# One PSUM operand in each pass of the norm chain, and new orders on all five engines

## The chip, the cores and the metric

The kernel runs on one core of a Trainium2 chip. The metric is the device time of one launch in microseconds; the time before is the median of three runs. All data is fp32 but for a few bf16 tables and parts.

## The reference, cut to what matters

The first part is a global attention over x of 8 sequences x 512 tokens x 128 channels, whose result is added at the end. The change leaves it alone but for one shared helper. The second part, called the layers here, takes most of the time. It applies the following to each of the 8 sequences, six times over with other weights:

```
# one layer, x: 512 tokens x 128 channels, 16 heads of 64
t    = shift_tokens(x)                 # the upper 64 channels come from the token before
q,k,v = split(t @ Wqkv)
q    = rotary(q / |q| * q_scale) ; k = rotary(k / |k| * k_scale)
sim  = 8 * q k^T                       # windows of 32 tokens look at themselves and the window before
attn = softmax(masked sim)
x    = x + (attn v) @ Wo
xn   = (x' - mean(x')) / sqrt(var(x') + 1e-5) * g + b       # x' = shift_tokens(x)
a, gate = split(xn @ W1 + b1)
x    = x + (a * gelu(gate)) @ W2 + b2
```

Each token needs 32 reciprocal norms (16 heads of q and 16 of k) and one reciprocal standard deviation: 512 tokens on 128 partitions make 4 x 32 + 4 = 132 numbers on a partition. They are computed in one go by a start value from integer arithmetic on the float's bits and three Newton steps. This is the norm chain.

## The kernel before, in words

The layers run on items: item n is sequence n mod 8 in layer n div 8, so there are 48. Every engine runs the same software pipeline. Its program is a `body` that is written out for i = -1 to 51 by `bodies`; x_0 is item i, x_1 item i - 1 and so on to x_4, and x_ahead is item i + 1. A stage of the work on an item is a small function, and a body is a list of such calls: this list, written out by hand for each engine, is the order in which the engine takes its work. An engine never takes work out of this order. All dependencies are semaphores.

An item passes these stages; the names are those of the functions, the letter is the engine (P TensorE, V VectorE, A ScalarE, G GpSimd, S SyncE).

- `tokens` (A) copies x and its shifted half to xs. `project` (P, L922) has 16 tiles of q and k, 4 for each of the 4 units (a unit is 4 heads), into the two buffers of pj_ps. Each tile is squared by `squares` (A, L1219), then multiplied by the gain and both rotary tables by `products` (V, L1092), which frees the buffer. `rotate` (G, L1317 and L1318) joins products to rotated queries or keys.
- `square_sums` (P, L932) adds up squares by head in the first 128 columns of nq_ps. `copy_sums` (A), `sums_by_token` (P, L940, a transpose), and `variance` of the item three before (P, L946) prepare the 132 numbers per partition in nq_ps. `norms` (V, L1105) adds eps and calls `rsqrt` (L58 to L65), eleven passes that each wait for the one before.
- `widen_norms` (A), `spread_norms` (P, L960) and `scale_keys` (V, L1118) multiply the keys by their reciprocal norms. `queries` and `keys` (S) rearrange both by DMA. `scores` (P, L971), `mask_scores` and `score_maxima` (V), `less_max` and `scale_scores` (G, L1322 and L1329), `exponentials` (A, L1236), `prob_sums` (V), `normal_probs` (G) and `prob_blocks` (V, a block transpose) make the probabilities of a unit.
- `token_transposes` (P) and `copy_tokens` (A) prepare x by token. `attend` (P, L991) runs on four groups of 128 tokens, `take_u` (A, L1250) copies the eight results, and `combine` (P, L1003) applies the product of value and output weights for 16 heads into to_ps. `attention_sum` (V, L1152) adds it to x.
- `ffn_tokens` (A), `centred` (P), `centred_squares` (A), `variance`, then a later run of the norm chain, `spread_rstd` (P, L953) and `normalise` (V, L1113). `up` (P, L1020), `gates` (A, L1270, Gelu), `gated` (V, L1158) for three chunks, `down` (P, L1027) and `ffn_sum` (V, L1165).

Everything that TensorE gives to others besides projections, sums and to_ps goes through the two slots of pair_ps, taken in turns in TensorE's order: `slot` waits until the reader of the work two before in this ring has freed it. attend takes both. to_ps is one buffer for combine and down. u is one buffer, so that take_u of an item waits for the last head of the item before. Exp and Gelu lie in different tables of ScalarE, and a load stands in the program wherever the one follows the other; squares and copies do with either.

In TensorE's order before, combine stands whole (heads 0 to 15 among projects) in one body, and after sums_by_token and variance comes attend 0 of the next item, so that two projects, attend 1 and project 2 are what it has while VectorE is in the norm chain.

## Time and profile before

| | |
|---|---|
| median of 3 runs | 3736.9 us (3736.53 to 3740.85) |
| profiled execution | 3733.54 us, span 3731.8 us |
| TensorE, VectorE, ScalarE, GpSimd busy | 92%, 80%, 49%, 58% of the span |
| mean granted TensorE clock | 0.980 |
| transposes of sums (L940), once an item | first at 561.0 us, last at 3574.8 us |

The span is from the first instruction to the last. Busy times are shares of it. In the timeline a row is one or several equal instructions in succession: the start, the length, the engine and line, output and input, their number, and in brackets how long the engine was idle before it and who released it. TensorE's matmuls overlap, so the distance between two starts is what counts there.

### The profile page before, as it was taken

How to read it: one execution, taken by the hardware profiler on the slowest of the kernel's cores; microseconds unless marked ns; L12 is line 12 of the kernel's file. 1: busy time of each engine (PE TensorE's matmuls, PEld its weight loads, DVE VectorE, ACT ScalarE, POOL GpSimd, SP SyncE). 2: the span in 40 equal slices, each digit the busy share in tenths (PEclk: the TensorE clock that was granted, in tenths of full speed). 3: DMA queues.
4: the chain of work that ended last, by engine and by line, in shares of the span. 5: the costliest groups of instructions: out<-in, count | busy, mean ns of one | idle time of the engine just before them, and what ended most of it. 6: DMA issues, size and time to landing. Idle time of an engine off the chain costs nothing. (4 is left out here: it accounts for less than half of the span.)

```text
span 3731.8 us, 75598 instructions
## 1 busy us (share of the span) xinstructions
PE 3415.4 (92%) x30012; PEld 1688.8 (45%) x30012; DVE 2966.9 (80%) x3289; ACT 1832.7 (49%) x2692; POOL 2171.0 (58%) x1534
## 2 busy tenths in 40 slices
PE   5888876999999999999999999999999999999986
PEld 3222223445454545545454545545454545445443
DVE  6788847888888888888888888888888888888862
ACT  2577753454545445454545454454545454454532
POOL 2322225757666675757576666757676666667550
PEclk7899998999999999999999999999999999999998
DMA  6222132323232323333232323233332323232221
GB/s 203 72 51 59 34 99 65 72 65 73 69 78 68 81 60 71 72 80 75 63 75 68 75 69 81 63 69 75 80 76 60 77 65 77 70 79 65 65 50 46
DMA packets 178253, 270.37 MB, mean 72 GB/s; under 512 B 42480, under 2 KB 67184, under 8 KB 176240
## 3 DMA queue, kind: packets, MB, share of 16 engines
q1 hardware_dynamic: 174160, 251.10, 29.0%
q10 hardware_dynamic: 3744, 14.43, 1.1%
q8 instruction: 242, 3.96, 0.5%
q14 instruction: 107, 0.88, 0.1%
HBM read 44.49 MB, written 19.55 MB: 17 GB/s over the span
## 5 line engine op out<-in xcount | busy, mean ns | idle before, releaser
L1092 DVE SCALAR_TENSOR_TENSOR ly_prod<-ly_pj_ps,ly_few,ly_tables 128x1024 f32<-128x1024 f32 x768 | 955.9, 1271 | 225.3 <-ACT ly_sq L1219 220.4
L922 PE MATMUL ly_pj_ps<-ly_xs,ly_wqk 128*128 128x512 f32 x1536 | 804.0, 621 | 103.8 <-DVE ly_prod L1092 91.4
L1219 ACT ACTIVATE ly_sq<-ly_pj_ps 128x512 f32<-128x512 f32 x768 | 454.7, 600 | 883.9 <-PE ly_pj_ps L922 591.2
L1003 PE MATMUL ly_to_ps<-ly_u,ly_mvo 128*128 128x512 f32 x1536 | 725.3, 596 | 0.9 <-DVE x_all L1165 0.9
L1250 ACT COPY ly_u<-ly_pair_ps 128x1024 f32<-128x1024 f32 x384 | 373.8, 1013 | 396.2 <-PE ly_pair_ps L991 396.2
L1322 POOL TENSOR_TENSOR ly_sx<-ly_sx,ly_smax 128x1024 f32<-128x1024 f32 x192 | 365.2, 1902 | 239.7 <-DVE ly_smax L1132 239.6
L1317 POOL TENSOR_TENSOR ly_qr<-ly_prod 128x512 f32<-128x512 f32 x192 | 244.2, 1272 | 425.5 <-DVE ly_prod L1092 420.5
L922 PEld LDWEIGHTS ly_pj_ps<-ly_xs,ly_wqk 128*128 128x128 f32 x1536 | 261.5, 191 | 499.3 <-issue 271.7
L1334 POOL TENSOR_TENSOR ly_sx<-ly_sx,ly_rsum 128x1024 f32<-128x1024 f32 x192 | 363.2, 1902 | 166.8 <-DVE ly_rsum L1140 166.8
L1003 PEld LDWEIGHTS ly_to_ps<-ly_u,ly_mvo 128*128 128x128 f32 x1536 | 280.5, 190 | 310.2 <-issue 310.2
L991 PE MATMUL ly_pair_ps<-ly_pt,ly_xt 32*128 32x512 f32 x3072 | 389.0, 620 | 25.7 <-ACT ly_u L1250 12.8
L971 PEld LDWEIGHTS ly_pair_ps<-ly_kbd,ly_qp 128*32 128x32 f32 x12288 | 325.6, 110 | 160.7 <-issue 157.9
L971 PE MATMUL ly_pair_ps<-ly_kbd,ly_qp 128*32 128x128 f32 x12288 | 376.7, 275 | 14.7 <-DMA ly_kbd<-ly_kr 14.6
L1329 POOL TENSOR_TENSOR ly_sx<-ly_sx,ly_rn 128x1024 f32<-128x1024 f32 x192 | 365.2, 1902 | 28.4 <-POOL ly_sx L1322 1.3
L1317 POOL TENSOR_TENSOR ly_kr<-ly_prod 128x512 f32<-128x512 f32 x192 | 247.3, 1288 | 209.1 <-DVE ly_prod L1092 206.2
L606 ACT ACTIVATE ga_pt<-ga_s_ps 128x512 f32<-128x512 f32 x512 | 276.9, 595 | 112.9 <-PE ga_s_ps L332 112.9
L466 DVE TENSOR_REDUCE ga_mx<-ga_f_ps 128x2 f32<-128x1024 f32 x256 | 302.5, 1220 | 35.9 <-PE ga_f_ps L312 34.8
L1020 PE MATMUL ly_pair_ps<-ly_xn,ly_w1c 128*128 128x512 f32 x576 | 288.8, 625 | 29.5 <-DVE ly_xn L1113 21.6
L1125 DVE TENSOR_TENSOR ly_sx<-ly_pair_ps,ly_mask 128x1024 f32<-128x1024 f32 x192 | 234.5, 1221 | 76.6 <-PE ly_pair_ps L971 76.5
L1236 ACT ACTIVATE ly_sx<-ly_sx 128x1024 f32<-128x1024 f32 x192 | 203.6, 1061 | 175.3 <-POOL ly_sx L1329 174.8
L1138 DVE TENSOR_REDUCE ly_rsum<-ly_sx 128x16 f32<-128x1024 f32 x192 | 233.5, 1216 | 61.3 <-ACT ly_sx L1236 58.3
L1118 DVE TENSOR_TENSOR ly_kr<-ly_kr,ly_pair_ps 128x1024 f32<-128x1024 f32 x192 | 233.5, 1216 | 21.7 <-PE ly_pair_ps L960 21.7
(112 smaller groups left out, 4259.5 us busy)
## 6 DMA issues: line engine op xcount, KB each, us to landing
ly_qp<-ly_qr SPq DMA_DIRECT2D x768, 128.0 KB, 2.4
ly_kbd<-ly_kr SPq DMA_DIRECT2D x1536, 64.0 KB, 2.0
ga_parts_dram<-ga_parts SPq DMA_DIRECT2D x16, 384.0 KB, 2.3
ga_qs<-ga_parts_dram SPq DMA_DIRECT2D x96, 64.0 KB
ga_ks<-ga_parts_dram SPq DMA_DIRECT2D x96, 64.0 KB
ly_wqk<-in_wqk SPq DMA_DIRECT2D x24, 256.0 KB, 3.4
ly_mvo<-mvo_dram SPq DMA_DIRECT2D x6, 1024.0 KB, 5.3
mvo_dram<-ga_pt ACTq DMA_DIRECT2D x4, 1024.0 KB, 4.0
```

The lines of the kernel that those rows point to most:

```text
L466: dve.tensor_reduce(mx[:, hp // 4, hp % 4, :, t], f_ps[:, k], AX.X, ALU.max).then_inc(max_done.sem, 1)
L922: pe.matmul(pj_ps[:, j % 2, :], wqk[:, g, j % TILES, :], xs[:, n % 2, WIN:], start=True, stop=True).then_inc(proj_ready.sem, 1)
L971: last = pe.matmul(pair_ps[32 * c:32 * c + 32, k, t // 2, at:at + 128], qp[:, g, p, WIN * w:WIN * w + WIN], kbd[:, g % 2, p, :, WIN * w:WI ...
L991: mm = pe.matmul(pair_ps[:, ks[c // 2], c % 2, :], xt[rows, late, t, :], pt[rows, t, :, late, :], start=(late == 0), stop=(late == 1), ski ...
L1003: last = pe.matmul(to_ps[:], mvo[:, h, :], u[:, :, :, h, :].rearrange("p t c q -> p (t c) q"), start=(h == 0), stop=(h == LH - 1))
L1092: dve.scalar_tensor_tensor(prod[:, k], pj_ps[:, j % 2, :].unsqueeze(1).to_broadcast([P, 2, N]), gains[:, n // B, k:k + 1], tables[:, table ...
L1219: act.activation(sq[:, k, :], pj_ps[:, j % 2, :], ACT.Square).then_inc(sq_done.sem, 1)
L1250: act.copy(u[:, k // 2, at:at + 2].rearrange("p c h q -> p c (h q)"), pair_ps[:, where["u", n, k]]).then_inc(u_copied.sem, 1)
L1317: pool.tensor_tensor(dst[:, 0], low[:, 0], high[:, 1], ALU.subtract).then_inc(rot_done.sem, 1)
L1322: pool.tensor_tensor(sx[:, g % 2], sx[:, g % 2], smax[:, g % 2].unsqueeze(3).to_broadcast([P, T, 4, SPAN]), ALU.subtract).then_inc(s_less. ...
L1329: pool.tensor_tensor(sx[:, g % 2], sx[:, g % 2], rq.unsqueeze(3).to_broadcast([P, T, 4, SPAN]), ALU.mult).then_inc(s_scaled.sem, 1)
L1334: pool.tensor_tensor(sx[:, g % 2], sx[:, g % 2], rsum[:, g % 2].unsqueeze(3).to_broadcast([P, T, 4, SPAN]), ALU.mult).then_inc(p_ready.sem, 1)
```

## The change

`rsqrt` computes t = y*x, t = -0.5*t*y, y = (t + 1.5)*y in place of t = y*y, t = -0.5*t*x, y = (t + 1.5)*y. The sums and the scratch t are no longer SBUF tiles but columns of nq_ps, so that of the operands x, t and y only y lies in SBUF. The waits of TensorE before it writes nq_ps are moved from the chain's first step to its last. And the bodies of all five engines have new orders. On TensorE, combine is cut: heads 0 to 4 close the body, heads 5 to 15 are in the next one, where the item is called x_3; attend 0 stands behind head 15. On ScalarE exponentials 0 stand between gates 1 and gates 2.

```diff
 def rsqrt(...):
-        eng.scalar_tensor_tensor(t, y, 1.0, y, ALU.mult, ALU.mult).then_inc(steps.sem, 1)
+        eng.tensor_tensor(t, y, x, ALU.mult).then_inc(steps.sem, 1)
         eng.wait_ge(steps.sem, steps.at(batch, n + 3 * i + 2))
-        eng.scalar_tensor_tensor(t, t, -0.5, x, ALU.mult, ALU.mult).then_inc(steps.sem, 1)
+        eng.scalar_tensor_tensor(t, t, -0.5, y, ALU.mult, ALU.mult).then_inc(steps.sem, 1)
...
-        ss = sb("ss", [P, NRN])
-        rt = sb("rt", [P, NRN])
+        sq_sums, rt = nq_ps[:, P:P + NRN], nq_ps[:, 272:272 + NRN]
...
 # square_sums, sums_by_token (and variance, with n + LATE - 1)
-                    pe.wait_ge(steps.sem, steps.at(n - 1, 1))
+                    pe.wait_ge(steps.sem, steps.at(n - 1, STEPS))
...
 # SyncE's body
-                if x_1 is not None: next_wqk(x_1, 3)
-                if x_0 is not None: queries(x_0, 0)
-                if x_1 is not None: keys(x_1, 1)
-                if x_0 is not None: next_wqk(x_0, 0)
-                if x_1 is not None: keys(x_1, 2)
-                if x_4 is not None: next_up(x_4)
-                if x_0 is not None: queries(x_0, 1)
-                if x_1 is not None: keys(x_1, 3)
-                if x_0 is not None: queries(x_0, 2); queries(x_0, 3)
-                if x_2 is not None: next_mvo(x_2)
-                if x_0 is not None: next_wqk(x_0, 1); next_wqk(x_0, 2); keys(x_0, 0)
+                if x_1 is not None: keys(x_1, 0); keys(x_1, 1)
+                if x_3 is not None: next_mvo(x_3)
+                if x_0 is not None: queries(x_0, 0)
+                if x_1 is not None: keys(x_1, 2)
+                if x_0 is not None: queries(x_0, 1)
+                if x_1 is not None: keys(x_1, 3)
+                if x_0 is not None: next_wqk(x_0, 0); next_wqk(x_0, 1); queries(x_0, 2)
+                if x_4 is not None: next_up(x_4)
+                if x_0 is not None: next_wqk(x_0, 2); queries(x_0, 3); next_wqk(x_0, 3)
```

TensorE's new body, in the order of the calls (the number behind a name is the tile, unit, group, chunk or head):

```
project(x_0, 0, 1); combine(x_3, 5, 6, 7, 8); spread_norms(x_1, 0); spread_rstd(x_4); combine(x_3, 9, 10)
project(x_0, 2); spread_norms(x_1, 1); combine(x_3, 11, 12, 13, 14); project(x_0, 3); combine(x_3, 15)
attend(x_2, 0); project(x_0, 4); square_sums(x_0, 0); attend(x_2, 1); project(x_0, 5); scores(x_1, 0); up(x_4, 0)
project(x_0, 6, 7); attend(x_2, 2); square_sums(x_0, 1); project(x_0, 8); spread_norms(x_1, 2); up(x_4, 1)
scores(x_1, 1); spread_norms(x_1, 3); project(x_0, 9); centred(x_3); project(x_0, 10); attend(x_2, 3)
project(x_0, 11, 12); up(x_4, 2); scores(x_1, 2); square_sums(x_0, 2); project(x_0, 13); down(x_4)
project(x_0, 14, 15); scores(x_1, 3); square_sums(x_0, 3); token_transposes(x_1)
sums_by_token(x_0); variance(x_3); combine(x_2, 0, 1, 2, 3, 4)
```

VectorE's, ScalarE's and GpSimd's (shortened to the names):

```
VectorE: mask 0, maxima 0 (x_1), gated 0 (x_4), products 6 7, keys 2, products 8, gated 1, mask 1, keys 3,
  products 9 10, maxima 1, sums 0, products 11, gated 2, blocks 0, mask 2, products 12 13, maxima 2, sums 1,
  products 14 15, ffn_sum (x_4), blocks 1, mask 3, maxima 3, norms, sums 2, products 0 (x_ahead), keys 0 (x_0),
  normalise (x_3), sums 3, products 1, blocks 2, keys 1, blocks 3 (x_1), attention_sum (x_2), products 2 3 4 5
ScalarE: gates 0 (x_4), squares 6 7, take_u 4 5 (x_2), squares 8, gates 1, exponentials 0 (x_1), squares 9,
  centred_squares (x_3), squares 10, take_u 6 7, squares 11, gates 2, squares 12 13, exponentials 1,
  squares 14 15, copy_sums, tokens, copy_tokens (x_1), exponentials 2, squares 0 (x_ahead), widen 0 (x_0),
  exponentials 3, widen 1, squares 1 2 3, widen 2, take_u 0 1 (x_1), squares 4, ffn_tokens (x_2), take_u 2,
  squares 5, take_u 3, widen 3
GpSimd (its body runs one item ahead): normal_probs 3 (x_1), rotate 3,1 (x_0), rotate 0,0 and 0,1 (x_ahead),
  less_max 0 (x_0), rotate 1,0, scale_scores 0, rotate 1,1, less_max 1, normal_probs 0, rotate 2,0,
  scale_scores 1, rotate 2,1, normal_probs 1, less_max 2, scale_scores 2, rotate 3,0, less_max 3,
  scale_scores 3, normal_probs 2
```

## Rows read from the trace of the kernel before

**Rows 1.** Page, part 1: busy time, share of the span, instructions.
```profile
PE 3415.4 (92%) x30012; PEld 1688.8 (45%) x30012; DVE 2966.9 (80%) x3289; ACT 1832.7 (49%) x2692; POOL 2171.0 (58%) x1534
```
**Rows 2.** Timeline of TensorE: start, length; the transposes of items 4 and 47.
```profile
812.48 0.27 PE L940 MATMUL ly_nq_ps<-ly_ident,ly_nsum 128*128 128x128 f32 x1
...
3574.77 0.27 PE L940 MATMUL ly_nq_ps<-ly_ident,ly_nsum 128*128 128x128 f32 x1
```
**Rows 3.** Windows: length, PE, PEld, DVE, ACT, POOL busy, clock, DMA share, GB/s.
```profile
1200.00:1600.00 400.00, 384.23 (x3476) 197.40 (x3468) 332.84 (x358) 199.55 (x278) 260.04 (x172) 1.00 0.31 71
```
**Rows 4.** Timeline of TensorE, one steady item.
```profile
1776.34 0.27 PE L940 MATMUL ly_nq_ps<-ly_ident,ly_nsum 128*128 128x128 f32 x1
...
1777.33 2.00 PE L991 MATMUL ly_pair_ps<-ly_pt,ly_xt 32*128 32x512 f32 x16
1779.26 1.98 PE L922 MATMUL ly_pj_ps<-ly_xs,ly_wqk 128*128 128x512 f32 x4
1781.44 2.00 PE L991 MATMUL ly_pair_ps<-ly_pt,ly_xt 32*128 32x512 f32 x16 [0.19 <-ACT ly_u L1250]
1784.80 1.13 PE L922 MATMUL ly_pj_ps<-ly_xs,ly_wqk 128*128 128x512 f32 x2 [1.36 <-DVE ly_prod L1092]
...
1786.20 0.60 PE L960 MATMUL ly_pair_ps<-ly_ident,ly_rnx 128*128 128x128 f32 x4
1787.24 1.96 PE L1020 MATMUL ly_pair_ps<-ly_xn,ly_w1c 128*128 128x512 f32 x4 [0.43 <-DVE ly_xn L1113]
1789.47 1.12 PE L922 MATMUL ly_pj_ps<-ly_xs,ly_wqk 128*128 128x512 f32 x2 [0.28 <-DVE ly_prod L1092]
...
1792.46 1.12 PE L922 MATMUL ly_pj_ps<-ly_xs,ly_wqk 128*128 128x512 f32 x2
1793.62 1.98 PE L1020 MATMUL ly_pair_ps<-ly_xn,ly_w1c 128*128 128x512 f32 x4
1795.59 1.96 PE L971 MATMUL ly_pair_ps<-ly_kbd,ly_qp 128*32 128x128 f32 x64
...
1838.04 2.84 PE L1003 MATMUL ly_to_ps<-ly_u,ly_mvo 128*128 128x512 f32 x6
1840.72 0.27 PE L940 MATMUL ly_nq_ps<-ly_ident,ly_nsum 128*128 128x128 f32 x1
```
**Rows 5.** Timeline of VectorE: the norm chain of the same item and what follows.
```profile
1777.52 0.30 DVE L1105 SCALAR_TENSOR_TENSOR ly_ss<-ly_nq_ps,ly_eps 128x132 f32<-128x132 f32 x1 [0.28 <-PE ly_nq_ps L946]
1777.85 0.71 DVE L58 SCALAR_TENSOR_TENSOR ly_rn<-ly_ss,ly_few 128x132 int32<-128x132 int32 x1
1778.60 1.24 DVE L61 SCALAR_TENSOR_TENSOR ly_rt<-ly_rn 128x132 f32<-128x132 f32 x1
...
1781.15 0.29 DVE L65 SCALAR_TENSOR_TENSOR ly_rn<-ly_rt,ly_rn 128x132 f32<-128x132 f32 x1
...
1783.46 1.28 DVE L1092 SCALAR_TENSOR_TENSOR ly_prod<-ly_pj_ps,ly_few,ly_tables 128x1024 f32<-128x1024 f32 x1
1784.66 0.68 DVE L1152 TENSOR_TENSOR x_all<-ly_to_ps,x_all 128x512 f32<-128x512 f32 x1
```
**Rows 6.** Timeline of GpSimd beside that norm chain.
```profile
1778.36 1.33 POOL L1317 TENSOR_TENSOR ly_kr<-ly_prod 128x512 f32<-128x512 f32 x1
1779.64 1.32 POOL L1318 TENSOR_TENSOR ly_kr<-ly_prod 128x512 f32<-128x512 f32 x1
```
**Rows 7.** Timeline of ScalarE: the square of the project at 1784.80.
```profile
1785.96 0.60 ACT L1219 ACTIVATE ly_sq<-ly_pj_ps 128x512 f32<-128x512 f32 x1
```
**Rows 8.** Groups by line, 1200 to 3500 us: busy, mean ns | idle before.
```profile
L1322 POOL TENSOR_TENSOR ly_sx<-ly_sx,ly_smax 128x1024 f32<-128x1024 f32 x144 | 273.9, 1902 | 169.3 <-DVE ly_smax L1132 169.2
```
**Rows 9.** The same view: the table loads of ScalarE.
```profile
L1270 ACT ACT_TABLE_LOAD x36 | 46.2, 1283 | 0.6
L1236 ACT ACT_TABLE_LOAD x36 | 46.2, 1283 | 0.6
```
**Rows 10.** Timeline of SyncE's queue: the eight DMAs of one unit's keys.
```profile
1817.15 4.98 SPq L858 DMA_DIRECT2D ly_kbd<-ly_kr  x8
```

More of the change, by code:

```diff
@@ L1031, in body @@
                 if x_0 is not None: project(x_0, 0, 1)
+                if x_3 is not None: combine(x_3, 5, 6, 7, 8)
+                if x_1 is not None: spread_norms(x_1, 0)
+                if x_4 is not None: spread_rstd(x_4)
+                if x_3 is not None: combine(x_3, 9, 10)
+                if x_0 is not None: project(x_0, 2)
+                if x_1 is not None: spread_norms(x_1, 1)
+                if x_3 is not None: combine(x_3, 11, 12, 13, 14)
+                if x_0 is not None: project(x_0, 3)
@@ L1032, in body @@
+                if x_3 is not None: combine(x_3, 15)
+                if x_2 is not None: attend(x_2, 0)
+                if x_0 is not None: project(x_0, 4); square_sums(x_0, 0)
                 if x_2 is not None: attend(x_2, 1)
-                if x_0 is not None: project(x_0, 2)
-                if x_4 is not None: spread_rstd(x_4)
-                if x_1 is not None: spread_norms(x_1, 0)
+                if x_0 is not None: project(x_0, 5)
+                if x_1 is not None: scores(x_1, 0)
@@ L1036, in body @@
                 if x_4 is not None: up(x_4, 0)
-                if x_0 is not None: project(x_0, 3)
+                if x_0 is not None: project(x_0, 6, 7)
                 if x_2 is not None: attend(x_2, 2)
-                if x_0 is not None: project(x_0, 4)
+                if x_0 is not None: square_sums(x_0, 1); project(x_0, 8)
+                if x_1 is not None: spread_norms(x_1, 2)
                 if x_4 is not None: up(x_4, 1)
-                if x_1 is not None: scores(x_1, 0)
-                if x_0 is not None: square_sums(x_0, 0)
@@ L1043, in body @@
-                if x_1 is not None: spread_norms(x_1, 1)
+                if x_1 is not None: scores(x_1, 1); spread_norms(x_1, 3)
+                if x_0 is not None: project(x_0, 9)
                 if x_3 is not None: centred(x_3)
-                if x_0 is not None: project(x_0, 5)
+                if x_0 is not None: project(x_0, 10)
                 if x_2 is not None: attend(x_2, 3)
-                if x_0 is not None: project(x_0, 6)
+                if x_0 is not None: project(x_0, 11, 12)
@@ L1048, in body @@
                 if x_4 is not None: up(x_4, 2)
-                if x_0 is not None: project(x_0, 7)
-                if x_1 is not None: spread_norms(x_1, 2)
-                if x_0 is not None: project(x_0, 8)
+                if x_1 is not None: scores(x_1, 2)
+                if x_0 is not None: square_sums(x_0, 2); project(x_0, 13)
                 if x_4 is not None: down(x_4)
-                if x_1 is not None: scores(x_1, 1)
-                if x_0 is not None: square_sums(x_0, 1)
-                if x_1 is not None: spread_norms(x_1, 3)
@@ L1066, in body @@
-                if x_2 is not None: combine(x_2, 7, 8, 9)
-                if x_0 is not None: project(x_0, 14)
-                if x_2 is not None: combine(x_2, 10, 11)
-                if x_0 is not None: project(x_0, 15)
-                if x_2 is not None: combine(x_2, 12)
-                if x_0 is not None: square_sums(x_0, 3)
-                if x_2 is not None: combine(x_2, 13, 14, 15)
+                if x_0 is not None: project(x_0, 14, 15)
+                if x_1 is not None: scores(x_1, 3)
@@ L1073, in body @@
+                if x_0 is not None: square_sums(x_0, 3)
+                if x_1 is not None: token_transposes(x_1)
                 if x_0 is not None: sums_by_token(x_0)
                 if x_3 is not None: variance(x_3)
-                if x_1 is not None: attend(x_1, 0)
+                if x_2 is not None: combine(x_2, 0, 1, 2, 3, 4)
             bodies(body)
@@ L1195, in _ @@
+                if x_3 is not None: normalise(x_3)
+                if x_1 is not None: prob_sums(x_1, 3)
+                if x_ahead is not None: products(x_ahead, 1)
+                if x_1 is not None: prob_blocks(x_1, 2)
+                if x_0 is not None: scale_keys(x_0, 1)
+                if x_1 is not None: prob_blocks(x_1, 3)
+                if x_2 is not None: attention_sum(x_2)
+                if x_ahead is not None: products(x_ahead, 2, 3, 4, 5)
             bodies(body)
@@ L1272, in body @@
             def body(i, x_ahead, x_0, x_1, x_2, x_3, x_4):
-                if x_1 is not None: widen_norms(x_1, 2)
+                if x_4 is not None: gates(x_4, 0)
+                if x_0 is not None: squares(x_0, 6, 7)
+                if x_2 is not None: take_u(x_2, 4, 5)
+                if x_0 is not None: squares(x_0, 8)
                 if x_4 is not None: gates(x_4, 1)
-                if x_0 is not None: squares(x_0, 4)
+                if x_1 is not None: exponentials(x_1, 0)
+                if x_0 is not None: squares(x_0, 9)
@@ L1292, in body @@
-                if x_ahead is not None: squares(x_ahead, 0, 1)
-                if x_0 is not None: widen_norms(x_0, 0)
-                if x_1 is not None: take_u(x_1, 2, 3)
-                if x_ahead is not None: squares(x_ahead, 2)
-                if x_0 is not None: widen_norms(x_0, 1)
-                if x_3 is not None: gates(x_3, 0)
+                if x_1 is not None: copy_tokens(x_1); exponentials(x_1, 2)
+                if x_ahead is not None: squares(x_ahead, 0)
+                if x_0 is not None: widen_norms(x_0, 0)
@@ L1302, in _ @@
+                if x_ahead is not None: squares(x_ahead, 5)
+                if x_1 is not None: take_u(x_1, 3)
+                if x_0 is not None: widen_norms(x_0, 3)
             bodies(body)
```

104 lines of the change are left out of this document (47 added, 57 removed).

## The prediction

> **What bounds the kernel now.** I read the page's busy line first: TensorE is busy 92% of the span, VectorE 80%, GpSimd 58%, ScalarE 49% [rows 1]. The last is an average over three stages, so I went on to the layers alone. There the work repeats once for each of 48 items (6 layers by 8 sequences), and the transpose of the sums (L940), which runs once in an item, is a good clock: it starts at 812.48 for the fifth item and at 3574.77 for the 48th [rows 2]. So an item takes (3574.77 - 812.48) / 43 = 64.24 us, and the 43 steady items are 2762 us of the 3731.8. In a steady stretch of 400 us, that is 6.227 items, TensorE is busy 384.2, VectorE 332.8, ScalarE 199.6 and GpSimd 260.0 us at a granted clock of 1.00 [rows 3], or 61.7, 53.5, 32.0 and 41.8 us an item. TensorE is the bound, but 2.5 us an item is idle outright, and more is lost where a weight load comes late and the matmul record only looks longer.
>
> One item on TensorE's timeline shows where [rows 4]. I take the distance from start to start, not the duration. Unhindered, two project tiles take 1.72 (0.86 each: three combine heads from 1838.04 to 1840.72 are 2.68, so 0.86 to 0.89 each too), one attend 1.93, an up pair 1.82 to 1.86. Against that: the second attend starts 2.18 after its projects and not 1.72 (loss 0.46); the project at 1784.80 starts 3.36 after an attend of 1.93 (1.43, released by a product of VectorE); the first up starts 1.04 after a spread of 0.49 (0.55); it and the next project are 2.23 apart instead of 1.82 (0.41); the second up comes 1.16 after a 0.86 project (0.30) and takes 1.97 (0.15), and the third up loses 0.31 in the same way. That is 3.6 us an item. 64.38 between two transposes (1776.34 to 1840.72 here) less 3.6 leaves 60.8, the time an item would take with the same matmuls and no wait. The largest of these losses, 1.43 + 0.55 + 0.41, stand behind VectorE's norm chain.
>
> **The change, part by part.** First the norm chain (L1105 and the function at L58 to L65). On VectorE it runs from 1777.52 to 1783.46, 5.94 us for 11 small instructions [rows 5]. Those that nothing disturbs take 0.29 to 0.30 and come every 0.33; but L58 took 0.71, L61 1.24 and L63 behind it as much, just while GpSimd ran two rotations of 1.33 and 1.32 from 1778.36 to 1780.96 [rows 6]. When those are over, the same lines are back at 0.29 (L65 at 1781.15, and all after it). The stalled ones have two tensor operands in SBUF, and L1105, which reads one of them from PSUM, took 0.30 with GpSimd just as busy. The change gives every pass one PSUM operand, so 11 x 0.33 = 3.6 us: 2.3 us less, if the destination in PSUM costs nothing. Bounds: no pass reads or writes both sides as the new ones do here, so it may be anywhere from 3.6 to the old 5.94; I take 3.6, by L1105, the nearest row. TensorE's waits on the chain's first step (count 1) are now on its last (STEPS); they are those of square_sums, sums_by_token and variance, which come 15 us or more after it, with nothing queued up behind them that waits: nil. If the cover failed, it would cost the 3.3 us between first and last pass.
>
> The Trainium skill (SBUF — State Buffer, section "SBUF: two separate sides") says that a VectorE op with two SBUF inputs and a GpSimd op that reads SBUF exclude each other for whole instructions. By that the passes go to 0.30 each; the rows above agree with 1.24 beside 1.33.
>
> Second, the orders. No instruction is added on TensorE, VectorE, GpSimd or SyncE; the DMAs per item stay 16 for queries and 32 for keys. On TensorE the order is new in one large point: combine is deferred. Its heads 0 to 4 now stand right after variance, and 5 to 15 of the same item between the projects and spreads of the next body; attend 0 moves from the body's end to behind head 15. So while VectorE does the norms TensorE has heads 0 to 4, project 0 and 1 and heads 5 to 8 (9 x 0.86 + 1.72 = 9.5 us) before spread_norms needs the result, where before it had attend 0, two projects and attend 1 (5.9 us with its tight buffers).
>
> I laid out one body with the start-to-start figures of rows 4, zero at project 0, and put beside each step what it waits for. On VectorE each pass over 1024 columns counts as the product from 1783.46 to 1784.66 [rows 5], 1.20: 16 products and 20 others (masks, maxima, sums, blocks, keys) are 43.2, with 5.9 for the norms and some 5 for small ones 54, and rows 3 give 53.5. On ScalarE a square starts 1.16 after its project began (1784.80 to 1785.96 [rows 4, 7]; 1.05 where it has no wait before it), and the copies of u end 3 and 3.95 after the attend, as the 4.1 between two attends has it. A GpSimd pass over the scores is 1.90 [rows 8], a rotation 2 x 1.27. Without waits: spread 0 at 5.2, project 2 at 7.8, spread 1 at 8.8, project 3 at 12.7, head 15 at 13.6, attend 0 at 14.5, and the body ends at 61.0 (the 60.8 and two more changes between kinds of matmul of 0.1 each). With waits:
> - VectorE reaches the norms behind the fourth maxima, 1.7 us before the body's end, and is through at 1.9 of the next; the widening is done at 2.7, spread 0 wants it at 5.2. Cover 2.5 us.
> - It then does sums 2, product 0, keys 0 (waits for spread 0, done 7.2), normalise, sums 3, product 1, blocks 2, keys 1, blocks 3, done 13.9. Attend 0 needs this at 14.5. Cover 0.6 us: the thinnest.
> - attention_sum waits for head 15 and ends at 15.3, product 2 behind it at 16.5; project 4 needs that and could start at 16.4: 0.15 lost. Queued behind attention_sum are products 2 to 5; nobody else waits.
> - attend 0 and attend 1 can't be closer than 4.1 us (both copies of u; 1777.33 to 1781.44 in rows 4). Between them stand now 1.93 + 0.95 + 1.01 = 3.9: 0.1 lost where 0.46 is lost now.
> - scores 0 needs the buffer of attend 1's first half, whose copy stands on ScalarE behind square 4 and ffn_tokens: 0.35 lost.
> - centred waits for mask 1 and its product: 0.2 lost. Everything later had 0.1 to 5 us to spare.
> Sum 61.0 + 0.15 + 0.1 + 0.35 + 0.2 = 61.8. The three ups, which lose 1.7 now, lose nothing: no copy of u stands just ahead of them but in one case (0.4 to spare).
>
> Third, ScalarE. In the old order the three gates of an item follow each other with no exponential between them, so the 36 items of a steady stretch have 36 + 36 table loads of 1283 ns [rows 9]. In the new order exponentials 0 stand between gates 1 and gates 2: gates 0, 1, load, exp 0, load, gates 2, load, exp 1 to 3, load. That is two more loads, 2.57 us an item and 123 us in all, on an engine with 64.24 - 32.0 = 32 us of idle time. In the walk the second load ends 1.3 us after square 11 and delays gates 2 and through it only VectorE's third gated product, where blocks 0 waits for GpSimd until later anyway. I take 0 of it as lost; bounds 0 and 2.57 an item.
>
> The Trainium skill (ScalarE: Activation LUTs, section "Table sets: the hidden batching unit") speaks against this edit: functions of different sets should be grouped. By the loads' own duration it would be the rival below, if ScalarE were on the path.
>
> Fourth, SyncE. 8 key DMAs take 4.98 us of its queue, so 0.62 each [rows 10]; an item's 48 are 30 of 61.8 us. Queries 0 now wait behind keys 1 and for scores 0, and land some 5 us later (4 x 0.62 to issue, about as long to land), near 28.6; GpSimd's second query rotation wants them at 28.1. That shifts scale_scores 0 by half a us; exponentials 0 wait for their table load longer than that. Keys 2 and 3 land 5 us ahead of their scores. Cost nil, 0.5 if the cover is gone.
>
> Filling and draining (the first four items, and the 157 us behind the last transpose of sums) hold the same work; the norms give 2 us back in each early item, while project 2 now stands behind spread 0, which costs about as much. Nil, with 10 us either way.
>
> **Sum.** 43 x (64.24 - 61.8) = 105; I take 61.9 for small slips, so 101 us. The profiled execution took 3733.5 (span 3731.8 and 1.7 around it), less 101 is 3632.5; the median of the runs is 3.4 above that execution, so **3636**.
>
> **Rivals.**
> A. The passes don't get faster (PSUM to PSUM is slow, or the lock is something else). Then the norms end 2.3 us later, blocks 3 at 16.2, and attend 0 slips by 1.7: 63.6 an item with the other slips, 3733.5 - 28 + 3.4 = 3709. For it: no row with a PSUM destination. Against: L1105.
> B. The table loads come onto the path. Both: 61.9 + 2.57 = 64.5, 43 x 0.2 = 10 us longer less some filling, 3740: no change. One of them: 63.2, 3692. For it: ScalarE feeds VectorE in order, and squares 12 and 13 stand behind gates 2. Against: its 32 us.
> C. Slower than before. VectorE arrives late at blocks 3. It has no idle time from the norms to attention_sum except the wait for spread 0, cover 0.6, and GpSimd's normal_probs and scale_scores (four in a row near the body's end, 1.9 each) release what it does there. Each us beyond 0.6 goes straight to attend 0. From 0.6 + 2.4 = 3.0 us late it is slower than now; one more such GpSimd piece and a 2.5 us rotation late, 4.4 us, gives 61.9 + 3.8 = 65.7 and 3736.9 + 43 x 1.46 = 3800. For it: VectorE has only 61.9 - 51.2 = 10.7 us of idle time. Against: my walk has GpSimd 0 to 1 us ahead at each of these places.
> D. Nothing is lost at all: 61.0 to 61.2, some 3600.
>
> **How the numbers follow.** Forecast 0.60 (its own range 3610 to 3665), A 0.11, B 0.11, C 0.10, D 0.08. The range from 3596 to 3712 leaves out C, half of B and the tail of D, and holds A. A measurement of this kernel can tell about 0.2% (7.5 us). Faster: 0.60 + 0.11 + 0.06 (one load) + 0.08 = 0.85; same 0.05 (both loads); slower 0.10.
>
> **What would show it.** L58 to L65 at 0.30 each while GpSimd runs, the chain 3.6 us long; the transposes of sums 61.9 apart; table loads four to an item, with ScalarE's busy time at 34.6 an item; no wait of the project for a product above 0.3 us on TensorE, and its largest waits at project 4, attend 1 and scores 0. I am wrong if the transposes are above 63 apart; a wait of attend 0 for VectorE's block transposes means A or C (told apart by the length of the norm chain), a wait for ScalarE's squares, with loads just ahead of them, B.

## The result, and the profile after

The changed kernel takes **3570.3 us** (median of 4 runs, 3563.6 to 3577.1), the kernel before in the same session 3738.7 (3736.5 to 3740.9): a ratio of 0.955, 95% interval 0.953 to 0.957. The forecast was 3636, with a range from 3596 to 3712; the measured time lies 26 us below that range. The direction and the mechanism of the norm chain held. The gain is 168 us where 101 were expected, and two terms of the sum, named at the end, account for most of the rest. The profiled execution took 3566.4 us, its span is 3564.6.

The page's busy line answers to [rows 1], the two transposes (now L937) to [rows 2], the window to [rows 3]:

```profile
PE 3361.7 (94%) x30012; PEld 1679.6 (47%) x30012; DVE 2840.3 (80%) x3289; ACT 1985.2 (56%) x2782; POOL 2161.7 (61%) x1534
```
```profile
778.40 0.27 PE L937 MATMUL ly_nq_ps<-ly_ident,ly_nsum 128*128 128x128 f32 x1
...
3405.28 0.27 PE L937 MATMUL ly_nq_ps<-ly_ident,ly_nsum 128*128 128x128 f32 x1
```
```profile
1200.00:1600.00 400.00, 399.34 (x3679) 209.74 (x3680) 333.42 (x379) 225.86 (x301) 279.57 (x185) 1.00 0.31 76
```

A steady item takes (3405.28 - 778.40) / 43 = **61.09 us** instead of 64.24, and TensorE is busy 399.3 of 400 us instead of 384.2. The 167.2 us of span are these: 43 x 3.15 = 135.4 in the steady items; 28.1 in the first four (from the first transpose to the fifth: 251.5 before, 223.4 after); 6.0 ahead of the first transpose; and -2.3 behind the last one (157.0, now 159.3). The 6.0 can't be told from scatter: the first transpose lay at 561.0 before and 555.0 after, and in the experiments, of both kernels, anywhere between 552.3 and 565.8.

TensorE's timeline of one item (start, length, engine and line, output and input), which answers to [rows 4]:

```profile
2061.30 0.27 PE L937 MATMUL ly_nq_ps<-ly_ident,ly_nsum 128*128 128x128 f32 x1
...
2066.60 1.88 PE L919 MATMUL ly_pj_ps<-ly_xs,ly_wqk 128*128 128x512 f32 x4
...
2071.75 0.60 PE L957 MATMUL ly_pair_ps<-ly_ident,ly_rnx 128*128 128x128 f32 x4
...
2080.88 2.00 PE L988 MATMUL ly_pair_ps<-ly_pt,ly_xt 32*128 32x512 f32 x16
2082.93 1.12 PE L919 MATMUL ly_pj_ps<-ly_xs,ly_wqk 128*128 128x512 f32 x2
2083.98 1.08 PE L929 MATMUL ly_nq_ps<-ly_sq,ly_heads 128*32 128x128 f32 x32
2084.99 2.00 PE L988 MATMUL ly_pair_ps<-ly_pt,ly_xt 32*128 32x512 f32 x16
2086.92 1.13 PE L919 MATMUL ly_pj_ps<-ly_xs,ly_wqk 128*128 128x512 f32 x2
2088.09 1.96 PE L968 MATMUL ly_pair_ps<-ly_kbd,ly_qp 128*32 128x128 f32 x64
...
2102.13 1.02 PE L919 MATMUL ly_pj_ps<-ly_xs,ly_wqk 128*128 128x512 f32 x2
2103.15 1.10 PE L1007 MATMUL ly_pair_ps<-ly_xf,ly_centre 128*128 128x512 f32 x2
```

Read it from start to start, as in the prediction. The three projects that now stand behind the norm chain begin without an idle gap; before, two of them began 1.36 and 0.28 us late. In 1200 to 3350 us no matmul of the layers stands in the list of TensorE's waits any more. What is left are 0.06 to 0.2 us at four places, which show only in the distances between starts: project 4 begins 2.05 behind an attend of 1.93, the two attends are 4.11 apart, scores 0 begin 1.17 behind a project where 0.86 and a change of kind (0.1) would do, and centred 1.02 behind a project where 0.96 would do.

VectorE's norm chain of the same item (answers to [rows 5]) and GpSimd beside it ([rows 6]):

```profile
2065.28 0.29 DVE L1095 SCALAR_TENSOR_TENSOR ly_nq_ps<-ly_nq_ps,ly_eps 128x132 f32<-128x132 f32 x1
2065.61 0.30 DVE L58 SCALAR_TENSOR_TENSOR ly_rn<-ly_nq_ps,ly_few 128x132 int32<-128x132 int32 x1
2065.94 0.30 DVE L61 TENSOR_TENSOR ly_nq_ps<-ly_rn,ly_nq_ps 128x132 f32<-128x132 f32 x1
...
2068.94 1.22 DVE L1128 TENSOR_REDUCE ly_rsum<-ly_sx 128x16 f32<-128x1024 f32 x1
...
2072.46 1.22 DVE L1108 TENSOR_TENSOR ly_kr<-ly_kr,ly_pair_ps 128x1024 f32<-128x1024 f32 x1 [0.89 <-PE ly_pair_ps L957]
...
2078.98 1.23 DVE L1136 STREAM_TRANSPOSE ly_pt<-ly_sx 128x1024 f32<-128x1024 f32 x1
```
```profile
2064.51 1.27 POOL L1312 TENSOR_TENSOR ly_qr<-ly_prod 128x512 f32<-128x512 f32 x1
2065.75 1.26 POOL L1313 TENSOR_TENSOR ly_qr<-ly_prod 128x512 f32<-128x512 f32 x1
2066.97 1.90 POOL L1317 TENSOR_TENSOR ly_sx<-ly_sx,ly_smax 128x1024 f32<-128x1024 f32 x1
```

GpSimd is busy from the first pass to the last, and no pass takes over 0.30 us; the chain is 3.66 us long (5.94 before). The last two rows of VectorE are its covers (a cover is the time by which a result is ready before it is needed): it waits 0.89 us for spread 0 before keys 0, and blocks 3 end at 2080.21, 0.67 us ahead of attend 0. ScalarE's table loads have doubled as the walk had it. The groups of 1200 to 3350 us (35 items; count, busy, mean ns) have 71 for L1229 and 70 for L1263, where one an item stood at each line in [rows 9]:

```profile
L1263 ACT ACT_TABLE_LOAD x70 | 89.8, 1283 | 1.2
```

### The profile page after: what moved, and what is told of

Same layout as the page of the kernel before. It is cut to its first block and busy times, and to the rows that moved or that the text cites. A ratio compares the mean times of both kernels' runs of the same rounds, so it can differ in the third digit from the quotient of the medians.

```text
span 3564.6 us, 75684 instructions
## 1 busy us (share of the span) xinstructions
PE 3361.7 (94%) x30012; PEld 1679.6 (47%) x30012; DVE 2840.3 (80%) x3289; ACT 1985.2 (56%) x2782; POOL 2161.7 (61%) x1534
## 5 line engine op out<-in xcount | busy, mean ns | idle before, releaser
L919 PE MATMUL ly_pj_ps<-ly_xs,ly_wqk 128*128 128x512 f32 x1536 | 788.2, 615 | 38.9 <-DVE ly_prod L1082 21.6
L1000 PE MATMUL ly_to_ps<-ly_u,ly_mvo 128*128 128x512 f32 x1536 | 701.1, 595 | 0.1
L1312 POOL TENSOR_TENSOR ly_kr<-ly_prod 128x512 f32<-128x512 f32 x192 | 245.3, 1278 | 75.7 <-DVE ly_prod L1082 72.3
L1017 PE MATMUL ly_pair_ps<-ly_xn,ly_w1c 128*128 128x512 f32 x576 | 278.4, 607 | 5.5 <-ACT ly_u L1243 4.6
L1229 ACT ACTIVATE ly_sx<-ly_sx 128x1024 f32<-128x1024 f32 x192 | 203.0, 1058 | 135.1 <-POOL ly_sx L1324 134.0
L1313 POOL TENSOR_TENSOR ly_kr<-ly_prod 128x512 f32<-128x512 f32 x192 | 245.1, 1276 | 0.0
```

Of the source, the lines that this page charges most:

```text
L919: pe.matmul(pj_ps[:, j % 2, :], wqk[:, g, j % TILES, :], xs[:, n % 2, WIN:], start=True, stop=True).then_inc(proj_ready.sem, 1)
L1000: last = pe.matmul(to_ps[:], mvo[:, h, :], u[:, :, :, h, :].rearrange("p t c q -> p (t c) q"), start=(h == 0), stop=(h == LH - 1))
L1312: pool.tensor_tensor(dst[:, 0], low[:, 0], high[:, 1], ALU.subtract).then_inc(rot_done.sem, 1)
```

## The experiments

### The orders alone, and the chain alone

The first is the changed kernel with the norm chain of before:

```diff
-        eng.tensor_tensor(t, y, x, ALU.mult)
+        eng.scalar_tensor_tensor(t, y, 1.0, y, ALU.mult, ALU.mult)
-        eng.scalar_tensor_tensor(t, t, -0.5, y, ALU.mult, ALU.mult)
+        eng.scalar_tensor_tensor(t, t, -0.5, x, ALU.mult, ALU.mult)
-        sq_sums, rt = nq_ps[:, P:P + NRN], nq_ps[:, 272:272 + NRN]
+        ss, rt = sb("ss", [P, NRN]), sb("rt", [P, NRN])
-                    pe.wait_ge(steps.sem, steps.at(n - 1, STEPS))
+                    pe.wait_ge(steps.sem, steps.at(n - 1, 1))
```

> The changed kernel with the norm chain put back to SBUF scratch and the old Newton order. Theory (the passes with two SBUF operands wait for whole GpSimd instructions, and the new orders have 0.6 us of cover behind the chain): in its new place the chain stands beside 6.3 us of GpSimd work in a row (rest of rotation 3,0, less_max 3, scale_scores 3), one pass per GpSimd instruction, so it is 8 us long and not 3.7, block transposes 3 come 4.5 us later, and an item is 64 to 65.5 us and not 61.1: about 3740, no gain over the kernel before. Rival (the orders bring the gain, the chain is covered by heads 0 to 8 of combine): 61.1 an item, 3570. Rival (chain stays at its old 5.9): 62.7 an item, 3640.

Measured: 3754.6 us, ratio 1.0043 (1.0028 to 1.0058), an item of 64.83 us. As expected, the new orders gain nothing by themselves; they lose a little (16 us, outside the scatter of the runs). The chain on VectorE:

```profile
2033.71 1.25 DVE L61 SCALAR_TENSOR_TENSOR ly_rt<-ly_rn 128x132 f32<-128x132 f32 x1
2034.99 1.88 DVE L63 SCALAR_TENSOR_TENSOR ly_rt<-ly_rt,ly_ss 128x132 f32<-128x132 f32 x1
2036.90 2.01 DVE L65 SCALAR_TENSOR_TENSOR ly_rn<-ly_rt,ly_rn 128x132 f32<-128x132 f32 x1
```

It is 7.9 us long, 2 more than in the kernel before, since the new orders put more of GpSimd's work beside it: three passes last 5.1 us together instead of 0.9. And TensorE's timeline has something that nobody expected, in two successive items:

```profile
2288.81 0.27 PE L938 MATMUL ly_nq_ps<-ly_ident,ly_nsum 128*128 128x128 f32 x1
...
2301.38 1.06 PE L958 MATMUL ly_pair_ps<-ly_ident,ly_rnx 128*128 128x128 f32 x4 [1.96 <-ACT ly_rnx L1226]
...
2303.08 2.79 PE L1001 MATMUL ly_to_ps<-ly_u,ly_mvo 128*128 128x512 f32 x4
...
2353.75 0.27 PE L938 MATMUL ly_nq_ps<-ly_ident,ly_nsum 128*128 128x128 f32 x1
...
2366.31 0.66 PE L958 MATMUL ly_pair_ps<-ly_ident,ly_rnx 128*128 128x128 f32 x4 [1.95 <-ACT ly_rnx L1226]
...
2367.24 1.88 PE L1001 MATMUL ly_to_ps<-ly_u,ly_mvo 128*128 128x512 f32 x4
```

In both, spread 0 begins 12.56 us after the transpose (10.45 in the changed kernel) and has waited 1.95. In the first, what follows runs slowly. The windows of another such item (length, busy times, then the granted clock):

```profile
2041.50:2045.50 4.00, 3.91 (x11) 2.37 (x12) 3.97 (x6) 2.00 (x4) 1.90 (x1) 0.57 0.02 4
2045.50:2050.00 4.50, 4.50 (x15) 2.29 (x14) 4.47 (x6) 0.60 (x1) 3.22 (x3) 1.00 0.44 103
```

TensorE's clock fell from 2.4 GHz to 1.2 behind the wait and was back 3.4 us later. The transposes give the price: 64.94 us for the item with the fall (2288.81 to 2353.75), 63.72 for the next without it (2353.75 to 2417.47). Of the 43 steady items 38 had the fall and took 64.9 to 65.3 us, and five had not and took 63.7. The wait was 1.94 to 1.97 us with and without it, so the wait alone does not decide it. So the 3.74 us that the old chain costs under the new orders are 2.1 of late spread, some 0.5 of small waits behind it (63.72 - 61.09 - 2.1), and about 1.1 of clock.

The second is the kernel before with the new chain, and nothing else (the same edits the other way round).

> The kernel before with the new norm chain alone (sums and scratch in PSUM, new Newton order, TensorE's waits on the last step), all old orders. Theory: the chain falls from 5.9 to 3.7, the waits of project 2, up 0 and project 3 shrink by 2.0 to 2.2 an item, so 62.0 to 62.3 an item, about 3640 (ratio 0.974). The waits of TensorE for copies of u stay. Rival (the order of attend and copies holds the same place, 4.1 between attends): under 0.7 an item, 3710. Rival (the waits on the last step cost): no change.

Measured: 3708.0 us, ratio 0.9918 (0.9901 to 0.9934), an item of 63.64 us. The chain is 3.67 us long, so it does what it does in the changed kernel; but the theory's gain (2.0 us an item or more) did not come, and the rival's (under 0.7) did: 0.6. The idle time of TensorE in the layers (line, waited for, total us, times, longest), of the kernel before and of this one:

```profile
PE ly_pj_ps L922 <- DVE ly_prod L1092: 52.6, 70, 1.4
```
```profile
PE ly_pj_ps L921 <- DVE ly_prod L1091: 23.3, 36, 0.7
PE ly_pair_ps L959 <- ACT ly_u L1249: 9.9, 34, 0.3
```

The wait for the product shrank by 29 us in 35 items; a new one for ScalarE's copies of u, which the old order sets in front of spread 0, takes a third of it back.

Against the 3738.2 us that the kernel before took beside these two, the orders give +16.4 and the chain -30.2 us, together -14; the whole gives -168. The halves need each other. The orders take TensorE off everything but the chain, and the chain then has to be short.

### SyncE's order alone

The kernel before with the new order of queries, keys and weight loads on SyncE (the diff of the change's SyncE part, nothing else).

> The kernel before with SyncE's new order alone (keys 1 no longer behind queries 0 of the next item). Theory: steady item unchanged at 64.24, since scores 1 don't wait for DMA there; in the first two items, where scores waited 10.6 us for keys by DMA, 3 to 8 us less. Rival (SyncE's queue accounts for all that the first four items gained): 28 us less there, ratio 0.992.

Measured: 3764.8 us, ratio 1.0068 (1.0049 to 1.0087), an item of 64.81 in the mean; the first four items are not shorter (253.6 us, 251.5 before). The mean hides two kinds of item: the middle one takes 64.2, as expected, and five take 66.7 to 68.8. The gain in the first items did not come, and a loss that neither theory nor rival had did. GpSimd's waits, kernel before and this one:

```profile
POOL ly_qr L1317 <- DMA ly_qp<-ly_qr: 0.7, 1, 0.7
```
```profile
POOL ly_qr L1315 <- DMA ly_qp<-ly_qr: 175.3, 31, 9.8
```

Nearly once in an item the rotation of queries waits for the transfer of the unit before. SyncE's queue stands at the keys placed ahead of those queries, which the old orders of the others finish late: in the item from 1725.79 it issues 16 keys in 17.0 us and only then the queries. Such a wait is 4.2 to 6.3 us long, and nearly all of these items take 64.2 to 64.8 all the same. The five long items, one in each of the layers 2 to 6, are the ones where it is 8.4 to 9.8 us. In them the new order has the load of combine's weights just ahead of the queries (issues of SyncE, then GpSimd):

```profile
1686.19 0.58 SPq L823 DMA_DIRECT2D ly_mvo<-mvo_dram  x1
1686.87 2.41 SPq L848 DMA_DIRECT2D ly_qp<-ly_qr  x4
```
```profile
1695.68 1.27 POOL L1315 TENSOR_TENSOR ly_qr<-ly_prod 128x512 f32<-128x512 f32 x1 [9.43 <-DMA ly_qp<-ly_qr]
```

These four transfers of queries land 6.1 to 6.9 us after their issue, where those of the next item take 2.3 to 2.5. TensorE then waits up to 2.8 us for a product, and in four of the five items its clock falls behind that wait. The five items are 19.5 us longer than 64.2 each, out of some 25 us lost in the 43. That the weight load is what delays the transfers was read from these rows, not tested. The changed kernel has the same load at the same place, and there no steady item is above 61.2. SyncE takes its list strictly in order, and its new list fits only the new lists of the others.

### Where the length of the chain begins to count

The changed kernel with only the scratch `t` back in SBUF:

```diff
-        sq_sums, rt = nq_ps[:, P:P + NRN], nq_ps[:, 272:272 + NRN]
+        sq_sums = nq_ps[:, P:P + NRN]
+        rt = sb("rt", [P, NRN])
```

> The changed kernel with the scratch t of the Newton steps in SBUF, the sums x still in PSUM. So L61 and L58 keep one PSUM operand, L63 and L65 read two SBUF operands. Theory (two SBUF operands are what stalls): only L63 and L65 stall, 1.2 to 1.9 each while GpSimd works, L58 and L61 stay at 0.30; the chain is 7 to 8 us and an item 64 to 65. Rival (it is the destination, or the chain was slow for another reason): all 0.30, 61.1 an item.

Measured: 3672.6 us, ratio 0.9823 (0.9808 to 0.9837), an item of 63.03.

```profile
2059.55 0.29 DVE L61 TENSOR_TENSOR ly_rt<-ly_rn,ly_nq_ps 128x132 f32<-128x132 f32 x1
2059.87 0.92 DVE L63 SCALAR_TENSOR_TENSOR ly_rt<-ly_rt,ly_rn 128x132 f32<-128x132 f32 x1
2060.82 1.88 DVE L65 SCALAR_TENSOR_TENSOR ly_rn<-ly_rt,ly_rn 128x132 f32<-128x132 f32 x1
...
2063.06 1.68 DVE L63 SCALAR_TENSOR_TENSOR ly_rt<-ly_rt,ly_rn 128x132 f32<-128x132 f32 x1
```

L61 still has x in PSUM and takes 0.29 every time; L63 and L65, whose operands are now both in SBUF, take up to 1.88. Which passes stall is exactly as expected; so it is the pair of SBUF operands, not the arithmetic, the type or the destination. This is the rule of the Trainium skill (SBUF — State Buffer, section "SBUF: two separate sides") that the prediction cited, and the trace agrees with it: 0.29 beside GpSimd with one operand in PSUM, up to 1.88 with both in SBUF. The chain is 7.2 us long, 3.5 longer than in the changed kernel, and the item 1.94: so some 1.6 us of the chain's length are free. That is why the expected 64 to 65 us were not reached. Spread 0 waits 1.25 us in the mean here (42.6 us in 34 times), so its own cover is 3.5 - 1.25 = 2.3 us; the kernel with the orders alone agrees (7.9 - 3.66 - 2.3 = 1.9, where it waits 1.95). The clock stays at 1.00 in all steady items.

To see that cover without touching the chain, one and then two idle reductions of 1.2 us were put behind it on VectorE, over the rotary tables, with nobody reading the results:

```diff
+                if k < ITEMS:
+                    for r in range(1):                      # 2 in the second kernel
+                        dve.tensor_reduce(idle[:, r], tables[:, 0:2, :]...).then_inc(idled.sem, 1)
```

> The changed kernel with one idle VectorE pass (a maximum over 1024 constant columns, 1.2 us, into scratch of its own) between the norm chain and sums 2 of every item. Theory from its trace: VectorE waits 0.89 us for spread 0 at keys 0, and block transposes 3 end 0.67 before attend 0, so 1.5 us of cover: the item stays at 61.1 (at most 61.3), the wait at keys 0 goes. Rival (no cover, VectorE and TensorE are equally the bound): +1.2, 62.3 an item, 3622.

> The same with two idle passes, 2.3 to 2.4 us. Theory (cover 1.5): +0.8 to +0.9, so 61.9 to 62.0 an item, about 3608, with attend 0 of TensorE waiting for VectorE's block transposes. Rival (no cover): +2.4, 63.4, 3673. Rival (VectorE catches up elsewhere): 61.1.

Measured: with one, 3571.8 us (0.9565, 0.9551 to 0.9579) and an item of 61.09, the changed kernel's own; with two, 3600.6 (0.9646, 0.9632 to 0.9661) and an item of 61.73. So 1.2 us are free, and of 2.4 us 0.64 arrive (0.8 to 0.9 were expected): a cover between 1.2 and 1.8 us. VectorE's two covers in the changed kernel, 0.89 before keys 0 and 0.67 behind blocks 3, add up to 1.56, for a late chain uses up its wait for spread 0 first. TensorE's only outright wait in the kernel with two:

```profile
PE ly_pair_ps L990 <- DVE ly_pt L1143: 20.6, 35, 0.7
```

It is attend 0, behind VectorE's block transposes: the place that the prediction called the thinnest, at 0.6.

### The table loads

The changed kernel with exponentials 0 behind gates 2, so that gates 0 to 2 and exponentials 0 to 3 are each together and an item has two loads, not four (ScalarE's list; the other lists stay):

```diff
                 if x_4 is not None: gates(x_4, 1)
-                if x_1 is not None: exponentials(x_1, 0)
...
                 if x_4 is not None: gates(x_4, 2)
+                if x_1 is not None: exponentials(x_1, 0)
```

> The changed kernel with exponentials 0 on ScalarE moved behind gates 2, so that all Gelu of an item stand together and table loads fall from four to two an item, 2.57 us less on ScalarE. Theory (ScalarE isn't the bound, VectorE's order is fixed and waits for exponentials 0 at sums 0): they come some 11 us later, VectorE stands 4 to 6 us at sums 0, has 1.5 of cover, and an item is 64 to 65.5 us, 3690 to 3755. Rival (the loads are on the path): 60.5 or less an item, under 3550.

Measured: 3751.6 us, ratio 1.0049 (1.0034 to 1.0064), an item of about 65.0: 181 us slower than the changed kernel, with 2.57 us an item less of loads. Grouping them in this way costs 4 us an item, as the theory had it. What the two extra loads cost in the changed kernel was not measured by itself; it can't be more than the 0.5 us an item of small waits that TensorE has left there. The waits show the way that the delay takes, first TensorE's, then VectorE's:

```profile
PE ly_pj_ps L919 <- DVE ly_prod L1082: 96.5, 57, 2.2
```
```profile
DVE ly_rsum L1128 <- ACT ly_sx L1229: 156.8, 33, 4.8
```

VectorE's list stands still for 4.8 us an item at the sums of probabilities (L1128), which wait for the late exponentials 0, and the products that TensorE's projects need stand behind it. The Trainium skill's rule (ScalarE: Activation LUTs, section "Table sets: the hidden batching unit"), by which calls should be grouped by the set of tables that they need, gives the wrong sign for this grouping, though a load lasts the same 1283 ns each time: ScalarE is idle for 26 us an item (226 of 400 us busy), and what counts is when each exponential ends.

### How far VectorE is behind TensorE

The changed kernel without the middle one of down's three products (a chunk of the feed-forward part is left out of the output):

```diff
                     pe.wait_ge(hid_done.sem, hid_done.at(n, c + 1))
...
+                    if c != 1:
                         last = pe.matmul(to_ps[:], w2[:, c, :], hid[:, c, :], ...)
```

> The changed kernel with the middle one of down's three products left out, 0.86 us of TensorE's work in each item. Theory (TensorE is the bound, the others have more than 0.86 to spare since VectorE waits 0.89 for spread 0): 60.2 to 60.3 an item, 40 us less in all. Rival (another engine's loop is as long): no more than 0.3 an item, 14 us. It leaves a third of the hidden channels of the feed-forward part out of its sum.

Measured: 3557.3 us, ratio 0.9524 (0.9508 to 0.954), an item of 60.71. Taking 0.86 us of TensorE's work away gains 0.38, where the theory had all of it and the rival at most 0.3; so the theory failed, and the rival was nearly right. The rest turns into waits for products; weight loads waiting for them, in the changed kernel and in this one:

```profile
PEld ly_pj_ps L919 <- DVE ly_prod L1082: 35.7, 67, 0.9
```
```profile
PEld ly_pj_ps L919 <- DVE ly_prod L1083: 84.9, 103, 0.9
```

So at this place the others, VectorE's list first by these waits, are only 0.4 us an item behind TensorE's. TensorE is the bound, by a small margin.

### An attempt at the rest of the waits, and at the end

Two tiles of project were put into the waits that the changed kernel has left, and, in another kernel, the final part's load of the sums was issued after the last scores, into the then dead tile of queries, with the layers' identity used again (in the first, the squares on ScalarE follow TensorE's order, and square 6 stands ahead of gates 0):

```diff
 # project first
-                if x_0 is not None: project(x_0, 5)
+                if x_0 is not None: project(x_0, 5, 6)
                 if x_1 is not None: scores(x_1, 0)
                 if x_4 is not None: up(x_4, 0)
-                if x_0 is not None: project(x_0, 6, 7)
+                if x_0 is not None: project(x_0, 7)
...
-                if x_0 is not None: project(x_0, 9)
+                if x_0 is not None: project(x_0, 9, 10)
                 if x_3 is not None: centred(x_3)
 # final part early, at the end of SyncE's list
+                if i == ITEMS:
+                    sp.wait_ge(s_ready.sem, s_ready.at(ITEMS - 1, UNITS))
+                    sp.dma_start(part, sum_dram).then_inc(fi_loaded, 16)
```

> The changed kernel, with two tiles of project put into the two waits that TensorE still has in a steady item: project 6 ahead of scores 0 (scores 0 began 1.17 us after project 5, where a tile takes 0.86) and project 10 ahead of centred (which began 1.02 us after project 9). The squares on ScalarE follow that order. Theory, TensorE bounds the item and each wait counts: 0.3 + 0.15 us an item less, 60.65 us, and over 44 items about 20 us: near 3550. Rival, VectorE's own round is only 0.4 us behind TensorE's at the place where down's products were left out, so the work waits elsewhere: no more than 0.2 us an item, 3562 or more; and if the later scores 0 make mask 0 and the gates late, the item grows, 61.3 us and 3580.

> The changed kernel, with the final part's load of the sums (2 MB) issued after the last scores into the tile of queries, which is dead by then, and the layers' own identity used again, so that the final part waits for no transfer. Theory: in the changed kernel TensorE waits 12.3 us for the identity after the last item (its first transpose at 3553.41, ScalarE's copy ready at 3542.8), so the end comes 10 us earlier: 3560. Rival: the start of the last part is bound by its other steps or the early load delays the last keys: 3 us or less. The item stays at 61.09.

> Both edits together. Theory: the gains are at different places and add, about 30 us: near 3541. Rival: only the final part's 10 us count, 3560.

Measured: the first 3634.9 us (0.9733, 0.972 to 0.9746), **65 us slower** than the changed kernel, with an item of 62.48: theory wrong, and the rival right in sign but far too small (it had 0.2 us an item and 10 in all, and 1.4 and 65 came). The second 3561.7 (0.9535, 0.9522 to 0.9548), 9 us less than the changed kernel. Both together 3624.8 (0.9701, 0.9688 to 0.9714): the effects add, though neither the 3541 of the theory nor the 3560 of the rival came. TensorE in the first:

```profile
2065.33 1.96 PE L968 MATMUL ly_pair_ps<-ly_kbd,ly_qp 128*32 128x128 f32 x64
...
2070.63 2.00 PE L988 MATMUL ly_pair_ps<-ly_pt,ly_xt 32*128 32x512 f32 x16 [0.58 <-DVE ly_hid L1148]
...
2082.41 1.13 PE L919 MATMUL ly_pj_ps<-ly_xs,ly_wqk 128*128 128x512 f32 x2 [0.51 <-DVE ly_prod L1082]
```

Attend 2 takes both slots of the ring, so it needs mask 0 and the first gated product, which follow scores 0 on VectorE (that product begins 4.42 us behind scores 0 in both kernels). Project 6, moved from behind scores 0 to ahead of them, was the cover between; without it attend 2 waits, and what was won ahead of scores 0 is lost again. Project 11, moved ahead of attend 3, waits for product 9. A wait of 0.2 us in a list this tight was the visible end of a margin elsewhere. Which of the two moves costs more was not tried.

The early load shows at the end. Timeline of the changed kernel (the last sum, then the final part's first transposes), and of the kernel with the early load:

```profile
3541.15 0.75 DVE L1155 SCALAR_TENSOR_TENSOR x_all<-ly_to_ps,ly_few,x_all 128x512 f32<-128x512 f32 x1 [1.82 <-PE ly_to_ps L1024]
...
3553.41 3.60 PE L1389 MATMUL fi_tr<-fi_ident,fi_xt 128*128 128x128 f32 x16 [12.29 <-DMA fi_ident<-in_ident]
```
```profile
3546.50 0.75 DVE L1161 SCALAR_TENSOR_TENSOR x_all<-ly_to_ps,ly_few,x_all 128x512 f32<-128x512 f32 x1 [1.83 <-PE ly_to_ps L1030]
...
3548.22 1.18 PE L1393 MATMUL ly_pair_ps<-ly_ident,ly_sq 128*128 128x128 f32 x8 [1.75 <-ACT ly_sq L1384]
```

12.3 us between the two have become 1.7, and from the last sum to the end of the span it is 13.1 us instead of 23.4. By the whole time alone the two kernels are not told apart (the intervals 0.952 to 0.955 and 0.953 to 0.957 overlap), but in the trace the 10 us are plain.

## Why the prediction was right, and where it failed

The direction and the norm chain were right, and the time was 66 us too high. Two terms of the sum failed. The steady item was put at 61.9 us and takes 61.09, which makes 34 us; and "filling and draining: nil" missed 26 us. The last 6 us lie ahead of the layers, within the scatter shown above.

**The norm chain: right.** 3.6 us forecast, 3.66 measured, each pass at 0.30 with GpSimd busy throughout. A destination in PSUM costs nothing.

**The orders and their covers: right in place, partly in size.** The walk's offsets from project 0, against the trace: spread 0 at 5.2 (5.15), project 2 at 7.8 (7.74), spread 1 at 8.8 (8.60), project 3 at 12.7 (12.47), head 15 at 13.6 (13.33), attend 0 at 14.5 (14.28). Spread 0's cover was put at 2.5 us (2.3 by the experiments), attend 0's at 0.6 (0.67). The walk names VectorE's wait for spread 0 but does not count it as cover: a late chain uses it up first, so 1.56 us are free and not the 0.6 beyond which rival C sends each us "straight to attend 0".

**The term of the steady item: mis-sized by 0.8 us.** The forecast took 61.9, the item takes 61.09. Of the difference 0.3 are the four waits: 0.15 + 0.1 + 0.35 + 0.2 = 0.8 forecast, 0.12 + 0.10 + 0.20 + 0.06 = 0.5 measured. Another 0.1 is the "small slips", which did not come. The last 0.4 is the work without waits, 61.0 by the walk and 60.6 by the trace. The walk took 60.8 from one old item (1776.34 to 1840.72, 64.38 us) which was longer than most: 38 of the 43 steady items take 64.20 to 64.23, and 64.21 less the same 3.6 is 60.6, what the new item has. The 0.2 for changes of kind came on top. Over 43 items the 0.8 are 34 us. Rival D, "nothing is lost at all", was nearest to the steady items, and it was given 0.08.

**"Filling and draining: nil, 10 us either way": wrong, and the other half of the miss.** From the first transpose to the fifth, and behind the last one:

| kernel | first four items | behind the last | gain in both |
|---|---|---|---|
| before | 251.5 | 157.0 | |
| chain alone | 246.8 | 161.8 | 0 |
| orders alone | 235.0 | 168.3 | 5.2 |
| changed | 223.4 | 159.3 | 25.8 |

The single columns mislead: in the new order the 16 heads of combine (16 x 0.86 = 13.8 us) stand behind the transpose, not ahead of it, which moves 13.8 us from the first column to the second. Their sum is free of that. The kernel with one idle pass, whose steady item is the changed kernel's, has 226.1 + 158.9, a gain of 23.5, so the 25.8 are good to some 2 us. It shows the pattern of the steady items again: the orders alone give 5 us, the chain alone none, and under the new orders the short chain gives 20.6 more (with the scratch in SBUF the gain is 9.8: 231.9 + 166.7). The prediction set the 2 us that the norms give back in each early item against "project 2 now stands behind spread 0, which costs about as much"; a loss of that size did not come, and where in the early items the gain arises was not followed further. With the 6 us ahead of the layers this makes 32 us, and 34 + 32 are the 66 by which the forecast was too high.

**TensorE's waits on the last step, SyncE, table loads: right**, at nil each or too small to see: the list of TensorE's waits has none for any of them. For SyncE the reason was too weak: its order was costed by itself, and the experiment shows that it is part of one plan with the others; in the old plan it costs 27 us, most of it in five single items.

**The rivals.** A (the passes don't get faster) is refuted by the chain itself. Its price was too low by more than half (1.7 us an item for 3.7): with the old chain the new orders take 64.8 an item, not 63.6, for the chain grows to 7.9 us beside the new GpSimd order, and the clock falls behind the wait. B (table loads on the path) did not happen: an item of 61.09 leaves no room for 2.57 us, and the kernel with fewer loads is slower, though by its late exponentials. C (VectorE late at blocks 3) did not happen, but its place was the right one to fear.

## What to carry to other kernels

When TensorE is nearly full, cost the covers and not only the work: find each wait's slack by putting an idle pass of known length in front of it, and treat the visible 0.2 us gaps as the ends of chains, which a move of one tile can lengthen. Read the work of an item from one that has the usual length, and look at every item when a mean moves: five long ones made it here. A short dependent chain on VectorE should keep one operand of each pass in PSUM wherever GpSimd works beside it. Orders of several engines are one plan; a part of the plan moved into the old one tells what it needs, not what it is worth.

## What the runs showed of the hardware that was not expected

- A VectorE pass that reads one operand from PSUM and writes to PSUM ran at 0.30 us beside GpSimd, the same as one that writes SBUF. With both operands in SBUF the same pass took up to 2.01 us, the length of GpSimd's own instruction (1.90 to 1.95).
- A wait of 1.95 us on a TensorE that was otherwise full was followed, in 38 of 43 items, by a stretch at 1.2 GHz of 3.4 us, which cost 1.2 us of the item. In the kernel with gates together a wait of 2.18 us stood in every item and the fall came in only 11 of 43; there it cost 0.1 us (65.0 against 64.96), for TensorE had another wait of 1.0 us behind it, which the fall used up. Waits of 1.25 us in the mean, in the kernel with the scratch in SBUF, left the granted clock at 1.00.
- Transfers of queries issued just behind a load of weights landed after 6.1 to 6.9 us, others after 2.3 to 2.5.
